# A graph network kernel: the bias vector by one bf16 product, the degree one-hots and 37 weight loads at another place

## What is computed

```python
edge_index = jnp.stack([src, dst])
x = _layernorm(x + gcn(x, t_emb, edge_index, ...))                 # two GCN convolutions
x = _layernorm(x + gat(x, edge_index, W, att_src, att_dst, bias))  # attention, 4 heads, segment_max
x = _layernorm(x + attend(x, edge_attr_3, edge_weight1, ...))      # 8 heads, see below
x = _layernorm(x + message(x, edge_index, W_msg, b_msg, W_upd, b_upd))
```

## Time and profile before

| | us |
|---|---|
| median of 3 runs | 11539.33 |
| lowest, highest | 11539.1, 11558.92 |
| the profiled execution, its own time | 11537.76 |
| its span, first to last instruction | 11535.9 |

### The profile page before, as it was taken

One profiled execution on the slowest core, in us unless ns is written; L12 is line 12 of the kernel. 1 busy time (PEld: TensorE's weight loads), 2 busy tenths in 40 slices (PEclk: granted clock), 3 DMA queues, 4 the chain that ended last, 5 costly groups with the idle time before them and its releaser, 6 DMA issues. The chain is left out here.

```text
span 11535.9 us, 184986 instructions
## 1 busy us (share of the span) xinstructions
PE 7387.0 (64%) x39349; PEld 5638.8 (49%) x39350; DVE 8036.2 (70%) x21892; ACT 2653.4 (23%) x7536; POOL 5670.9 (49%) x5516
## 2 busy tenths in 40 slices
PE   4899980033333349798477772677557777777498
PEld 4777770022222235454477772666445555555344
DVE  8999991059999960202799997888668888887601
ACT  0111110000000000100244441222145655555100
POOL 0677777720000014070477777777337777777000
PEclk9555555555555569899555555777679999999699
DMA  1000000035555558586688886888823333335187
GB/s 40 2 2 2 2 2 2 2 111 157 157 158 158 157 171 311 186 320 218 186 273 273 272 269 199 258 257 260 158 82 107 107 108 107 107 108 100 13 306 251
DMA packets 1175179, 1718.20 MB, mean 149 GB/s; under 512 B 312964, under 2 KB 877024, under 8 KB 1137056
## 3 DMA queue, kind: packets, MB, share of 16 engines
q1 hardware_dynamic: 565184, 1048.17, 27.8%
q0 software_dynamic: 204496, 358.11, 12.8%
q10 hardware_dynamic: 405264, 309.21, 8.6%
HBM read 1290.72 MB, written 424.01 MB: 149 GB/s over the span
## 5 line engine op out<-in xcount | busy, mean ns | idle before, releaser
L1389 POOL DMA_INDIRECT big<-tab_h,idx x1728 | 2015.5, 1166 | 1060.0 <-issue 500.3
L2276 POOL DMA_INDIRECT big<-tab_kv,idx x1728 | 1648.4, 954 | 766.4 <-issue 504.8
L885 POOL DMA_INDIRECT by_src<-big,h x1568 | 1532.7, 977 | 495.4 <-issue 476.6
L1550 DVE SCALAR_TENSOR_TENSOR acc<-big,room,acc 128x1280 f32<-128x1280 f32 (+1 forms) x960 | 1388.6, 1521 | 116.5 <-DMA big<-cells 116.1
L1821 DVE COPY acc<-banks 128x448 f32<-128x448 f32 x18 | 11.2, 625 | 1568.1 <-PE banks L1790 1566.5
L1202 DVE SCALAR_TENSOR_TENSOR acc<-acc,h,banks 128x128 f32<-128x128 f32 x4094 | 1101.8, 343 | 0.1
L916 POOL DMA_DIRECT2D room<-by_src x9 | 5.2, 584 | 2205.2 <-POOLq L2570 2205.2
L1790 PE MATMUL banks<-big,h 128*128 128x448 f32 x2744 | 1036.4, 541 | 18.1 <-DMA big<-cells 18.1
L1673 PE MATMUL banks<-big 128*128 128x132 f32 x3456 | 682.7, 362 | 346.5 <-DVE acc L1698 343.5
L1523 PE MATMUL banks<-we2t,acc 128*128 128x8 f32 x3456 | 802.9, 361 | 0.0
L667 PE MATMUL banks<-room 50*128 50x100 f32 x3136 | 794.4, 432 | 0.0
(11 more groups left out here) (477 smaller groups left out, 13891.8 us busy)
## 6 DMA issues: line engine op xcount, KB each, us to landing
big<-cells SPq DMA_DIRECT2D x262, 1568.0 KB
cells<-acc SPq DMA_DIRECT2D x2049, 64.0 KB, 1.6
cells<-acc ACTq DMA_DIRECT2D x2048, 64.0 KB
big<-cells ACTq DMA_DIRECT2D x196, 640.0 KB, 5.6
head_rows<-big SPq DMA_DIRECT2D x432, 264.0 KB, 4.7
big<-head_rows SPq DMA_DIRECT2D x216, 528.0 KB
room<-w_rows SPq DMA_DIRECT2D x216, 512.0 KB, 4.3
big<-loc_rows SPq DMA_DIRECT2D x216, 256.0 KB
```

Of the source, the lines that this page charges most:

```text
L885: pool.indirect_dma_start(k.by_src_dram, bass.IndirectOffsetOnAxis(k.pos[:, t:t + 1], axis=0), k.src_rec[:, t, :], None).then_inc(self.sca ...
L1389: pool.indirect_dma_start(k.stage[:, m % BODY, :], None, k.tab_h_dram, bass.IndirectOffsetOnAxis(k.idx[:, m:m + 1], axis=0)).then_inc(k.ga ...
L1550: ins = dve.scalar_tensor_tensor(mine, strip, k.small_asrc[:, src, h:h + 1], mine, ALU.min, ALU.max)
L2276: pool.indirect_dma_start(far[:, m % (G * RING), 0:2 * C], None, k.tab_kv_dram, bass.IndirectOffsetOnAxis(k.idx[:, m:m + 1], axis=0)).then ...
```

## The change

Three parts.

1. The one-hots of the place within the block and their share of the product leave the count phase (`BOTH` goes, 178 becomes 50). A new class `Degrees` makes the degrees in the rank phase, on DVE and PE, between `stream` and `incidence`: again 98 rounds, each with a 50-wide and a 128-wide one-hot of 16 columns and 16 products of 50x128, with two buffers, in bank 7.
2. The 37 small loads leave the load phase. SP issues them at the start of the rank phase, `we2` first, with a semaphore of its own (`fetched`); PE waits for it before it turns `we2`.
3. In the maximum phase `be2` is split, by 17 small operations of DVE at the start, into three bf16 rows whose sum is the fp32 vector. The product that puts it into the bank is one of three rows in bf16 instead of one row in fp32.

```diff
@@ load_phase
-            for n in MATS:
-                load(k.w[n][:, :], a[n])
...
-            load(k.we1[:, :], a["L2_gnn_We1"])
-            load(k.we2[:, :], a["L2_gnn_We2"])
             sp.wait_ge(loaded, count[0])
@@ count_phase
                     one_hots(dve, k, hots[r][0], k.dhi_bf[:, at], NB1)
-                    one_hots(dve, k, hots[r][1], k.shi_bf[:, at], NB1)
-                    one_hots(dve, k, hots[r][1], k.dlo_bf[:, at], P, NB1).then_inc(made, 1)
+                    one_hots(dve, k, hots[r][1], k.shi_bf[:, at], NB1).then_inc(made, 1)
...
-                        last = pe.matmul(counts, column(hots[r][0], m, NB1), column(hots[r][1], m, BOTH),
+                        last = pe.matmul(counts, column(hots[r][0], m, NB1), column(hots[r][1], m, NB1),
                                          start=False, stop=False, skip_group_check=True)
@@ class Degrees, new
+    def vector(self, dve):
+        k = self.k
+
+        def body(i, first):
+            for r in range(2):
+                at = bass.ds((i * 2 + r) * ROUND_COLUMNS, ROUND_COLUMNS)
+                if not first:
+                    dve.wait_ge(self.taken, i * 2 + r - 1)
+                one_hots(dve, k, self.block[r], k.dhi_bf[:, at], NB1)
+                one_hots(dve, k, self.place[r], k.dlo_bf[:, at], P).then_inc(self.made, 1)
+        body(0, True)
+        with dve.Fori(1, TURNS // 2) as i:
+            body(i, False)
+        dve.wait_ge(self.summed, 1)
+        dve.tensor_copy(self.by_block, self.counts).then_inc(self.drained, 1)
+        dve.wait_ge(self.turned, 1)
+        dve.tensor_copy(k.deg[:, :], self.turn[:, 0:NB])
+
+    def tensor(self, pe):
...
+            for r in range(2):
+                pe.wait_ge(self.made, i * 2 + r + 1)
+                for m in range(ROUND_COLUMNS):
+                    ins = pe.matmul(self.counts, column(self.block[r], m, NB1), column(self.place[r], m, P),
...
+                ins.then_inc(self.taken, 1)
@@ rank_phase
+            sp.dma_start(k.we2[:, :], a["L2_gnn_We2"]).then_inc(fetched, 16)
+            for n in MATS:
+                load(k.w[n][:, :], a[n])
...
+            sp.wait_ge(fetched, 16)
+            sp.wait_ge(loaded, count[0])
             incidence.sync(sp)
...
+            pe.wait_ge(fetched, 16)
             pe.transpose(k.psum[7][:, 0:H2], k.we2[:, :], k.ident[0:H2, 0:H2]).then_inc(turned, 1)
             stream.tensor(pe)
             pe.wait_ge(stream.slotted, TURNS)
+            degrees.tensor(pe)
             incidence.tensor(pe)
...
             stream.vector(dve)
+            degrees.vector(dve)
             incidence.vector(dve)
@@ maximum_phase
-    level = k.acc[0:1, at:at + 4 * H2]
+    level = k.acc[0:3, at:at + 2 * H2].bitcast(BF16)
...
-                pe.matmul(mix[n % 2][:, 0:4 * H2], k.ones[0:1, :], level, start=True, stop=False, skip_group_check=True)
+                pe.matmul(mix[n % 2][:, 0:4 * H2], ones, level, start=True, stop=False, skip_group_check=True)
...
+            link(dve, dve.tensor_copy(rest, k.be2[0:3, :]))
+            for m in range(3):
+                link(dve, dve.tensor_copy(part_bf, rest))
+                link(dve, dve.tensor_copy(turn, part_bf))
+                link(dve, dve.tensor_tensor(rest, rest, turn, ALU.subtract))
+                link(dve, dve.tensor_scalar(turn, turn, k.ident[0:3, m:m + 1], None, ALU.mult))
...
```

More of the change, by code:

```diff
@@ L420, in count_phase @@
         hots.append([])
-        for width in (NB1, BOTH):
+        for width in (NB1, NB1):
             hots[r].append(k.chunk_room[:, at:at + width * 8].bitcast(BF16)
@@ L498, in _ @@
             pe.wait_ge(zeroed, 1)
-            pe.matmul(counts, none[:, 0:NB1], none[:, 0:BOTH], start=True, stop=False, skip_group_check=True)
+            pe.matmul(counts, none[:, 0:NB1], none[:, 0:NB1], start=True, stop=False, skip_group_check=True)
             with pe.Fori(0, TURNS // 2) as i:
@@ L864, in sync, with __init__, body @@
         sp.wait_ge(stored, 16)
+class Degrees:
+    def __init__(self, k):
+        self.k = k
+        self.made, self.taken, self.summed, self.drained, self.turned = (k.sem("degree_" + n) for n in (
+            "made", "taken", "summed", "drained", "turned"))
+        room, size = k.chunk_room, 8 * (NB1 + P)
+        hots = [room[:, r * size:(r + 1) * size] for r in range(2)]
+        self.block = [h[:, 0:8 * NB1].bitcast(BF16).rearrange("p (o c i) -> p o c i", o=8, i=2) for h in hots]
+        self.place = [h[:, 8 * NB1:size].bitcast(BF16).rearrange("p (o c i) -> p o c i", o=8, i=2) for h in hots]
+        self.by_block = room[0:NB1, 2 * size:2 * size + P]
+        self.counts, self.turn = k.psum[7][0:NB1, 0:P], k.psum[7][:, P:P + NB1]
+    def vector(self, dve):
[15 more added lines that the diff above has]
+    def tensor(self, pe):
+        k = self.k
+        def body(i, first, last):
+            for r in range(2):
+                pe.wait_ge(self.made, i * 2 + r + 1)
+                for m in range(ROUND_COLUMNS):
+                    ins = pe.matmul(self.counts, column(self.block[r], m, NB1), column(self.place[r], m, P),
+                                    start=first and not r and not m, stop=last and r == 1 and m == ROUND_COLUMNS - 1,
+                                    skip_group_check=True)
+                ins.then_inc(self.taken, 1)
+        body(0, True, False)
+        with pe.Fori(1, TURNS // 2 - 1) as i:
+            body(i, False, False)
+        body(TURNS // 2 - 1, False, True)
+        pe.wait_ge(self.taken, TURNS)
+        pe.sem_inc(self.summed, 1)
+        pe.wait_ge(self.drained, 1)
+        pe.transpose(self.turn, self.by_block, k.ident[0:NB1, 0:NB1]).then_inc(self.turned, 1)
@@ L941, in rank_phase @@
 def rank_phase(nc, k):
-    turned = k.sem("we2_turned")
-    scatter, stream, incidence = Scatter(k), Stream(k), Incidence(nc, k)
+    turned, fetched, loaded = k.sem("we2_turned"), k.sem("we2_fetched"), k.sem("weights_loaded")
+    scatter, stream, degrees, incidence = Scatter(k), Stream(k), Degrees(k), Incidence(nc, k)
+    a = k.a
     with nc.Block() as block:
@@ L1428, in maximum_phase @@
     at += 4 * 4 * H2
-    level = k.acc[0:1, at:at + 4 * H2]
+    level = k.acc[0:3, at:at + 2 * H2].bitcast(BF16)
+    at += 2 * H2
+    ones = k.acc[0:3, at:at + P // 2].bitcast(BF16)
+    at += P // 2
+    part, rest, turn = (k.acc[0:3, at + m * H2:at + (m + 1) * H2] for m in range(3))
+    part_bf = k.acc[0:3, at + 3 * H2:at + 3 * H2 + H2 // 2].bitcast(BF16)
     mix = (k.psum[6], k.psum[7])
@@ L1537, in _ @@
         def _(dve):
-            dve.tensor_copy(level.rearrange("o (w h) -> o w h", h=H2),
-                            k.be2[0:1, :].unsqueeze(1).to_broadcast([1, 4, H2])).then_inc(widened, 1)
+            link(dve, dve.tensor_copy(rest, k.be2[0:3, :]))
[4 more added lines that the diff above has]
+                link(dve, dve.tensor_scalar(turn, turn, k.ident[0:3, m:m + 1], None, ALU.mult))
+                if m:
+                    link(dve, dve.tensor_tensor(part, part, turn, ALU.add))
+                else:
+                    link(dve, dve.tensor_copy(part, turn))
+            dve.memset(ones, 1.0)
+            dve.tensor_copy(level.rearrange("o (w h) -> o w h", h=H2), part.unsqueeze(1).to_broadcast([3, 4, H2]))\
+                .then_inc(widened, 1)
             for m, (c, src) in enumerate(steps):
```

38 lines of the change are left out of this document (20 added, 18 removed).

## The result

The changed kernel takes 11379.62 us (median of four, 11371.24 to 11395.15) where the kernel before takes 11541.74 beside it: a ratio of 0.986, with a 95% interval of 0.9848 to 0.9873. The forecast was 11380. The sum was right, its terms less so: the load phase, the degree rounds and the maximum phase missed in both directions, two phases that were not in the sum moved, and all that cancelled. Of the attend phase's +5.3 a second profile of the same kernel shows only +1.9.

| phase | before | after | moved | forecast |
|---|---|---|---|---|
| load | 67.6 | 48.6 | -19.0 | -26 |
| count | 223.6 | 121.8 | -101.8 | -106 |
| rank | 2045.9 | 2080.1 | +34.2 | +62 |
| cells (behind rank) | 1825.8 | 1810.3 | -15.4 | 0 |
| maximum | 1621.2 | 1554.2 | -67.0 | -90 |

What follows compares the result with a forecast made beforehand. Each barrier-separated phase was bound by its own engine: SP in load, DVE in count, POOL in rank, a PE-ACT loop in most of maximum. Terms -26 - 106 + 62 - 90 = -160 us gave 11380 us, range 11335 to 11440.

Steps and rivals of the forecast that it cites:

- The load phase: Front of the kernel: with 37 small loads gone from SP's queue, DVE starts near 42 instead of 68 us, minus 26.
- the 38 to 42 us window: Load phase: DMA engines only 0.05 busy, read as table filling over by 42 and SP's small loads alone being late.
- Where the loads go: Start of the rank phase: 37 issues in SP's queue, PE's wait for we2 covered by POOL's iotas, cost 0.
- The count loop: Count phase without its 2048-element one-hot: 98 rounds fall from 2.11 to 1.03 us each, minus 106.
- The degree rounds: Rank phase behind the stream: 98 rounds of 1.90 us hold POOL to one scatter each instead of 1.27, plus 62.
- at the high clock ... plus 34: Rank phase alternative: with PE at the high clock a degree round takes DVE's own 1.62 us, costing 34 instead of 62.
- The rival of a POOL not held up: Rank phase tail: wide one-hots let scatters in at any time; sum -222, 11318 us, chance 0.09.
- The bias vector: Maximum phase: single-pass bf16 product cuts the loop from 6.40 to 5.88-5.54 us, DVE's 5.87 takes over, minus 90.
- no DVE wait of note after the first strip: Maximum phase, expected sign in the profile: DVE never waits notably after its first strip, with gathers 1.47 us apart.
- No gather phase changed its clock: Rival in a PE-bound gather phase: granted 1.2 GHz instead of 2.4, +520 us; sum +360, 11899 us, chance 0.04.
- the count loop's hand-offs: Count phase rival: longer hand-offs make rounds 1.35 us, saving 75 instead of 106; 11411 us, chance 0.07.
- Rival 2: Maximum phase gives little, DMA or port holding its pace: 11470 us, or 11425 with half the gain; chances 0.08 and 0.10.

Runs made afterwards that it cites:

- the thirds: Changed kernel with each degree round's 2048-element one-hot in three pieces, and 960 instead of 1024 gathers in the maximum phase: 11372.13 us, ratio 0.9857.
- the pause for POOL: Changed kernel where DVE, in the maximum phase, waits before every fourth strip until its own last instruction has ended: 11366.14 us, ratio 0.9844.
- the halves' kernel: Changed kernel with each degree round's 2048-element one-hot in two of 1024, and the 31 edge rows loaded as 16 and 240 pieces: 11425.65 us.
- run 32: Not a follow-up run: "run" is a verb here, the first degree rounds of the changed kernel execute 32 products in 3.58 us.

## Why the prediction was right, step by step

**The load phase** (-26 forecast, -19). The failing step is the reading of the 38 to 42 us window: I took a DMA share of 0.05 for an idle queue and ACT's fill as the next late thing. By the run with the rows spread it was one engine of sixteen, on which the 31-row pieces of the edge arrays and the end of the fill stood in a row, hidden until then by SP's small loads. The spread rows took the phase to 36.3.

**Where the loads go** (0 forecast). Right: rank phase 2045.0 with them and 2045.9 without.

**The count loop** (-106 forecast, -101.8). Right in kind; the round is just over 1.08, the upper end of the range of 0.98 to 1.09 and not its middle.

**The degree rounds** (+62 forecast, +34.2). The mechanism held exactly: one scatter a round. The round was mis-sized, 1.90 instead of 1.62, and with it the term: "at the high clock ... plus 34" was written beside it. I had taken PE's speed in the stream for that of the rounds behind it. The rival of a POOL not held up is refuted by the 1.32 us scatters, and by the thirds, where lengthening DVE's work shortened POOL's. The named section of the Trainium skill's "SBUF — State Buffer" is half right here. DVE, where it came first, did keep POOL out for the whole instruction. But a tensor_tensor does hold up a DMA that POOL issues, by 0.35 us each time (1.32 against 0.97). The section also says that an instruction of DVE with two SBUF inputs contends with one of GpSimd that reads SBUF. The scatter reads its offsets there (`h` in its row), so no run here tells whether that read or the generation of descriptors is held up.

**The bias vector** (-90 forecast, -67.0). The unit's saving was right (loop 6.40 to 5.55, inside 5.54 to 5.88), and DVE took over as the bound of the steady stretch, busy 990.80 of 1000 us:

```profile
5900.00:6900.00 1000.00, 643.36 (x3000) 614.37 (x3000) 990.80 (x720) 474.51 (x1605) 789.11 (x692) 0.51 0.92 296
```

What failed is "no DVE wait of note after the first strip": DVE running without a pause starved POOL. With the pause for POOL the phase is 1534.5, 87 under the 1621.2 of the kernel before; and between kernels that both have a starving gather, 1642 and 1554 to 1566, the part is worth 76 to 88. In the halves' kernel, which has no pause but whose long gather ended after 21.65 us, it is 1533.0. So the size of the phase's gain was right and a wait that the forecast did not have took 20 to 30 us of it.

**What the sum left out.** Cells -15.4 and attend +5.3. The first comes from where a loop stands in DVE's program; of the second the table shows only that such shifts move that phase by a few us; the 200 us of other kernels come with the instruction fetches. That terms wrong by 4 to 28 us added up to the measured total within 1 us is luck.

**The rivals.** No gather phase changed its clock; the count loop's hand-offs are 1.08 a round and not 1.35. Rival 2, a maximum phase that gives little, came a quarter true, by a mechanism that it did not name.

## What to carry to other kernels

A DMA share is a share of sixteen engines: 0.06 for long can be one engine working alone, and a DMA with a row count like the 31 here is the first suspect. Where POOL issues DMAs beside wide DVE instructions, place the ends of DVE's instructions where POOL's next one is due, with a margin, rather than making them shorter; and leave a pause in a long run of them. Before a phase that the diff doesn't touch is called noise, look whether its loops have moved in the program and how many packets the instruction queues move in it, and compare phase by phase: a right total can be made of wrong terms.

## What was not expected of the hardware

- **The starving gather.** Of some 940 gathers a profile that start while DVE works, nearly all last 0.94 us or end 0.82 us after the instruction that they met, whichever is later, with DVE's instructions back to back or not. But nine of the ten profiles without the pause have one gather that misses every end: 45 to 49 us in eight of them, 21.65 in the halves' kernel, where DVE began one instruction 0.07 us late. POOL had waited 2.1 us or more before each; others had too, and got in. Why that one doesn't stays open; the pause shows only what lets it in. With it, in four kernels, the gather at that place took 9.38 to 10.06 us.
- **The granted clock and PE's speed.** Through the stream the record has the granted clock at 0.50 (1.2 GHz) in the kernel before, behind a count loop at 1.00, and at 1.00 (2.4 GHz) in the changed one. PE's fp32 products in it are no faster (ns, before and changed):

```profile
L667 PE MATMUL banks<-room x3136: 417/417/533, 317.9 to 1704.0; 50*128 50x100 f32 x196
```

```profile
L649 PE MATMUL banks<-room x3136: 417/418/533, 197.2 to 1583.2; 50*128 50x100 f32 x196
```

  The higher record comes with the degree part: the mean granted clock of the whole run is 0.769 with that part alone, 0.704 with the bias or the loads alone. Why was not tried. The first degree rounds, at 1.00 in the record, run 32 products in 3.58 us, later ones 16 in 1.10.
- **The place of a loop.** The attend phase takes 2232 to 2432 us with its DVE loop at one place or another, the cells loop 0.25 us a turn or nothing. With the attend loop at 3654 or before, its phase has 22 packets of instruction fetches, from 3659 on 282 or 283. Why the boundary lies there, and why the pause is 3 to 4 us at 3659 to 3688 and 5 to 6 at 3718, stays open. The 0.25 us of the cells loop come without such fetches (4 packets of that queue in that phase of the kernel before, 5 of the changed one).
